# Layer 0's attention: probabilities and values in two f32r parts, products for two query tiles at once, and the queries' fourth partial sum by ScalarE and GpSimd

## The reference

```
w = (qw - 8) * repeat(scales, 128)
q, k, v = x @ w_q, x @ w_k, x @ w_v        # 32 query heads, 8 key/value heads, width 128
q, k = rope(q), rope(k)
scores = q @ k.T / sqrt(128), causal       # per head 1024 x 1024
attn = softmax(scores);  ctx = attn @ v
out = ctx @ w_o                            # summed over the heads
```

## Time and profile before

| | |
|---|---|
| median of 3 runs | 1751.47 us (1750.13 to 1751.73) |
| profiled execution | 1747.66 us |
| its span, first to last instruction | 1745.8 us |
| mean granted TensorE clock | 0.978 |
| busy PE / DVE / ACT / POOL | 95% / 67% / 60% / 43% |
| f32 products of values, L778 | 2304 passes, 299.2 us busy |

### The profile page before, as it was taken

How to read it: one execution, slowest core, us unless ns; L and a number is a source line. 1 busy time by engine, 2 the same in 40 slices (tenths; PEclk the granted TensorE clock), 3 DMA queues, 4 the chain that set the end, 5 groups by cost and what they waited for, 6 DMA issues and landing times. The chain is left out here.

```text
span 1745.8 us, 28527 instructions
## 1 busy us (share of the span) xinstructions
PE 1654.7 (95%) x10107; PEld 1337.1 (77%) x10123; DVE 1170.5 (67%) x2951; ACT 1044.1 (60%) x2261; POOL 747.5 (43%) x705
## 2 busy tenths in 40 slices
PE   4899999999999999999999799999988999999897
PEld 2699989999999989899988488878764555555476
DVE  5767677777777676777666743336777777776285
ACT  3477777877777777777777221114324666666553
POOL 3286585675856757567551300000352334321200
PEclk9999999999999999999999889999979999999998
DMA  6100000101010010000000512200230000000000
GB/s 195 38 14 24 26 25 20 31 13 38 13 31 25 19 37 13 25 19 25 13 19 7 166 46 70 68 1 19 84 83 13 1 1 1 1 1 1 1 19 31
DMA packets 75014, 55.82 MB, mean 32 GB/s; under 512 B 23502, under 2 KB 57998, under 8 KB 74874
## 3 DMA queue, kind: packets, MB, share of 16 engines
q1 hardware_dynamic: 73290, 53.21, 10.5%
q10 hardware_dynamic: 1584, 0.79, 0.2%
HBM read 51.88 MB, written 2.10 MB: 31 GB/s over the span
## 5 line engine op out<-in xcount | busy, mean ns | idle before, releaser
L778 PEld LDWEIGHTS psum<-a_probsT,a_v 128*128 128x128 f32 x2304 | 294.7, 191 | 25.6 <-issue 3.9
L778 PE MATMUL psum<-a_probsT,a_v 128*128 128x128 f32 x2304 | 299.2, 275 | 1.7 <-ACT a_probsT L988 1.6
L877 DVE CUSTOM_DVE_ANT_0 psum<-psum,a_keys_allowed 128x128 f32<-128x128 f32 (+7 forms) x256 | 195.7, 764 | 83.1 <-PE psum L78 74.5
L2109 ACT ACTIVATE a_probsT<-psum 128x512 f32<-128x512 f32 (+1 forms) x304 | 168.4, 588 | 106.1 <-PE psum L1976 67.4
L971 ACT ACTIVATE a_probs<-psum,a_neg_max 128x128 f32<-128x128 f32 (+7 forms) x256 | 190.7, 745 | 66.4 <-DVE a_neg_max L877 58.0
L980 ACT ACTIVATE a_probs<-a_probs,a_row_inv 128x128 f32<-128x128 f32 (+7 forms) x256 | 201.2, 786 | 27.8 <-DVE a_row_inv L884 27.6
L641 POOL TENSOR_TENSOR a_turned_pool<-a_q_sum,a_sine 64x512 f32<-64x512 f32 x62 | 79.3, 1279 | 286.8 <-DVE a_q_sum L863 285.6
L907 DVE TENSOR_TENSOR a_ctxT_lo<-psum,a_ctxT_hi 128x128 fp32r<-128x128 f32 x256 | 73.5, 287 | 172.7 <-ACT a_ctxT_hi L994 172.6
L988 ACT COPY a_probsT<-psum 128x512 f32<-128x512 f32 (+3 forms) x384 | 173.3, 488 | 18.8 <-PE psum L766 16.6
L897 DVE SCALAR_TENSOR_TENSOR a_sumT<-psum,a_scale_o,a_sumT 128x512 f32<-128x512 f32 x248 | 173.5, 741 | 0.9 <-PE psum L792 0.8
L766 PE MATMUL psum<-ident,a_probs 128*128 128x128 f32 x1152 | 168.9, 274 | 0.5 <-ACT a_vT L965 0.3
(11 more groups left out here) (394 smaller groups left out, 3891.3 us busy)
## 6 DMA issues: line engine op xcount, KB each, us to landing
a_raw_o<-in_L_attn_qw_o SPq DMA_DIRECT2D x32, 256.0 KB, 2.8
a_raw_q<-in_L_attn_qw_q SPq DMA_DIRECT2D x31, 256.0 KB, 3.6
mod1b_w<-in_L_wmod SPq DMA_DIRECT2D x4, 1024.0 KB, 6.2
mod0a_w<-in_L_wmod SPq DMA_DIRECT2D x3, 1024.0 KB, 12.8
mod0b_w<-in_L_wmod SPq DMA_DIRECT2D x3, 1024.0 KB, 7.5
f_raw<-in_L_ffn_down_w SPq DMA_DIRECT2D x10, 256.0 KB, 3.1
f_raw<-in_L_ffn_gate_w SPq DMA_DIRECT2D x10, 256.0 KB, 3.3
f_raw<-in_L_ffn_up_w SPq DMA_DIRECT2D x10, 256.0 KB, 3.6
```

The costliest lines, as they stand in the source:

```text
L778: last = nc.tensor.matmul(bank(use)[:, 0:P], v[:, g % 2, j, :], probsT[:, u % 2, j, :], start=(j == 0), stop=(j == i))
L877: nc.vector.tensor_tensor_reduce(out=scores, in0=scores, in1=keys_allowed[:, S - (i + 1) * P:S], scale=-1.0, scalar=-MASKED, op0=ALU.add, ...
L2109: nc.scalar.activation(probsT[:, s % SLOTS, hs[0]:hs[-1] + 1, first:HALF], scores_of(group, n, HALF - first), ACT.Exp).then_inc(exped.sem, 1)
```

## The change

Six things change in this phase:

1. Turned probabilities and v are kept as two f32r parts. ACT copies the high part of the turned probabilities, DVE subtracts it to get the low part (`low_probs`, new). The same is done for v (`high_v` on ACT, `take_v` on DVE).
2. The values of two query tiles are computed together: for pair m, the key tiles 0 to 2m are multiplied as split products 128 x 256 wide; the odd tile's own key tile is done as one f32 product (`own`, a copy of ACT's). The cast and split of values are 256 wide, four a head.
3. The order within a unit: values of a pair (odd units) and the transposes come before the partial products. On DVE the split of values and `low_probs(u-1)` come after `maximum(u+1)` and before the sums, and `invert(u+1)` behind them. On ACT the cast of values and the copy of turned probabilities come right after `exponential(u+1)`. Output products move to even units.
4. A bank of turned probabilities is now taken out when DVE has made the low part (`lowered`).
5. The fourth partial product (k = 3) of the queries from head 2 on is copied with its scale by ACT into `extra` (`take_extra`), and GpSimd adds it to the sum as a first pass of the rope. DVE sums k = 1 and 2 only.
6. To make room, keys and values share one raw buffer, v holds one group, `ctxT` three halves, and some small tiles lie in `sumT`. SP's order of loads follows.

The core of the diff:

```diff
-        return [(h - 1, p - 1), (h - 1, p)] if h > 0 and p % 2 else []
+        return [(h - 1, p), (h - 1, p + 1)] if h > 0 and p % 2 == 0 else []
...
+        if w in (1, 4) and g > 0:
...
+    def pair_due(u):
+        if u % 2 == 0 or u < 3:
+            return []
+        h, i = units[u - 3]
+        return [(h, i // 2)]
...
+        uses += [("pv", *pair) for pair in pair_due(u)]
+        if u > 0:
+            uses += [("t", *piece) for piece in pieces_of(*units[u - 1])]
...
+    by_act_too = lambda key, k: k == KT - 1 and key[0] == "q" and key[1] > 1
+    extras = [key for key, k in partials if by_act_too(key, k)]
...
+            raw = raw_v0 if (name, g) == ("v", 0) else raw_kv
+            if g == 1 and name == "k":
+                sp.wait_ge(*wk_made.of(0))
+            elif g:
+                sp.wait_ge(*(wv_made.of(g - 1) if name == "k" else wk_made.of(g)))
...
+            if key in extras:
+                engine.wait_ge(*extra_out.of(key))
+                compute.tensor_tensor(x, x, extra[:, :], ALU.add).then_inc(counter.sem, 1)
+                engine.wait_ge(*counter.of((key, "extra")))
...
+                if h % REP0 == 0 and g < LAST_GROUP:
+                    load_kv(sp, "v", g + 1)
+                if h % REP0 == 1 and g + 2 <= LAST_GROUP:
                     load_kv(sp, "k", g + 2)
...
                 if kind == "t":
-                    return turned_out.of(name)
+                    return lowered.of(name)
                 key, k = name
+                if key in extras and k == KT - 1:
+                    return extra_out.of(key)
...
+            def values(h, m):
+
+                g, use = h // REP0, ("pv", h, m)
                 wait_bank(use)
-                if h % REP0 == 0 and i % TPH == 0:
-                    pe.wait_ge(*v_taken.of((g, i // TPH)))
-                pe.wait_ge(*turned_out.of(pieces_of(h, i)[-1]))
-                for j in range(i + 1):
-                    last = nc.tensor.matmul(bank(use)[:, 0:P], v[:, g % 2, j, :], probsT[:, u % 2, j, :],
-                                            start=(j == 0), stop=(j == i))
-                last.then_inc(filled.sem, 1)
+                if h % REP0 == 0 and m % 2 == 0:
+                    pe.wait_ge(*v_taken.of((g, m // 2)))
+                pe.wait_ge(*lowered.of(pieces_of(h, 2 * m + 1)[-1]))
+                for j in range(2 * m + 1):
+                    split_products(nc.tensor, bank(use)[:, 0:2 * P], [part[:, j, :] for part in v_parts],
+                                   [part[:, j, :] for part in probsT], j == 0, False)
+                nc.tensor.matmul(bank(use)[:, P:2 * P], v[:, 2 * m + 1, :], own[:, :], start=False, stop=True
+                                 ).then_inc(filled.sem, 1)
...
+                for due in pair_due(u):
+                    values(*due)
+                if u > 0:
+                    turn_probs(u - 1)
                 for due in q_partials(h, p) + kv_partials(h, p):
                     partial(*due)
                 for due in outputs_due(h, p):
                     output(*due)
                 if v_turn(h, p):
                     turn_v(*v_turn(h, p))
-                if u > 1:
-                    values(u - 2)
-                if u > 0:
-                    turn_probs(u - 1)
...
+                tiles_of, turned = slice(b * TPH, (b + 1) * TPH), bank(use).rearrange("p (t d) -> p t d", t=TPH)
+                dve.wait_ge(*v_hi_out.of((g, b)))
+                nc.vector.tensor_copy(v[:, tiles_of, :], turned)
+                nc.vector.tensor_tensor(v_parts[1][:, tiles_of, :], turned, v_parts[0][:, tiles_of, :].bitcast(F32),
+                                        ALU.subtract).then_inc(v_taken.sem, 1)
...
+            def low_probs(u):
+                h, i = units[u]
+                for piece in pieces_of(h, i):
+                    first_key = piece[2] * TPH
+                    keys = slice(first_key, min(first_key + TPH, i + 1 - i % 2))
+                    turned = bank(("t", *piece))[:, 0:(keys.stop - keys.start) * P].rearrange("p (j q) -> p j q", q=P)
+                    dve.wait_ge(*turned_out.of(piece))
+                    nc.vector.tensor_tensor(probsT[1][:, keys, tile(i % 2)], turned, probsT[0][:, keys, tile(i % 2)].bitcast(F32),
+                                            ALU.subtract).then_inc(lowered.sem, 1)
...
+            invert(0)
             for u, (h, i) in enumerate(units):
                 p = u % NT
-                invert(u)
                 if u + 1 < len(units):
                     maximum(u + 1)
                 if u < 2:
                 for use in first_uses(u):
                     if use[0] == "vt":
                         take_v(*use[1:])
+                for due in pair_due(u):
+                    split_values(*due)
+                if u > 0:
+                    low_probs(u - 1)
+                if u + 1 < len(units):
+                    invert(u + 1)
                 for key, k in q_partials(h, p) + kv_partials(h, p):
-                    if k:
+                    if k and not by_act_too(key, k):
                         add_partial(key, k)
                 for due in outputs_due(h, p):
                     add_output(*due)
                 if v_turn(h, p):
                     take_v(*v_turn(h, p))
...
             def take_turned(u):
                 h, i = units[u]
                 for piece in pieces_of(h, i):
-                    c, use = piece[2], ("t", *piece)
-                    keys = min(TPH, i + 1 - c * TPH)
+                    first_key, use = piece[2] * TPH, ("t", *piece)
+                    keys = slice(first_key, min(first_key + TPH, i + 1))
                     act.wait_ge(*filled.of(use))
-                    nc.scalar.copy(probsT[:, u % 2, c * TPH:c * TPH + keys, :].rearrange("p j q -> p (j q)"),
-                                   bank(use)[:, 0:keys * P]).then_inc(turned_out.sem, 1)
-
...
+                    if i % 2 and keys.stop == i + 1:
+                        keys = slice(first_key, i)
+                        nc.scalar.copy(own[:, :], bank(use)[:, tile(i - first_key)])
+                    turned = bank(use)[:, 0:(keys.stop - first_key) * P].rearrange("p (j q) -> p j q", q=P)
+                    nc.scalar.copy(probsT[0][:, keys, tile(i % 2)], turned).then_inc(turned_out.sem, 1)
+
+            def high_values(h, m):
+                use, (n, columns) = ("pv", h, m), part_of_ctx(h, m)
                 act.wait_ge(*filled.of(use))
-                nc.scalar.copy(ctxT[0][:, h % 2, tile(i)], bank(use)[:, 0:P]).then_inc(ctx_hi.sem, 1)
+                nc.scalar.copy(ctxT[0][:, n, columns], bank(use)[:, 0:2 * P]).then_inc(ctx_hi.sem, 1)
...
+            def high_v(g, b):
+                use = ("vt", g, b)
+                act.wait_ge(*filled.of(use))
+                nc.scalar.copy(v_parts[0][:, b * TPH:(b + 1) * TPH, :], bank(use).rearrange("p (t d) -> p t d", t=TPH)
+                               ).then_inc(v_hi_out.sem, 1)
+
+            def take_extra(key):
+                _, n, b = key
+                act.wait_ge(*filled.of(("part", key, KT - 1)))
+                if extras.index(key):
+                    act.wait_ge(*pool_roped.of((extras[extras.index(key) - 1], "extra")))
+                nc.scalar.activation(extra[:, :], bank(("part", key, KT - 1))[:, :], ACT.Copy, scale=scale_of(key, KT - 1)
+                                     ).then_inc(extra_out.sem, 1)
...
                 for use in first_uses(u):
                     if use[0] == "part":
                         take_first(use[1])
+                    elif use[0] == "vt":
+                        high_v(*use[1:])
                     elif use[0] == "so":
...
+                for due in pair_due(u):
+                    high_values(*due)
+                if u > 0:
+                    take_turned(u - 1)
                 for key, k in q_partials(h, p) + kv_partials(h, p):
                     if k == 0:
                         take_first(key)
-                if u > 1:
-                    high_values(*units[u - 2])
-                if u > 0:
-                    take_turned(u - 1)
+                    elif by_act_too(key, k):
+                        take_extra(key)
```

More of the change, by code:

```diff
@@ L458, in layer0_attention_phase @@
     firsts = [use[1] for use in uses if use[0] == "part" and use[2] == 0]
-    added_partials = [partial for partial in partials if partial[1]]
+    by_act_too = lambda key, k: k == KT - 1 and key[0] == "q" and key[1] > 1
+    extras = [key for key, k in partials if by_act_too(key, k)]
+    added_partials = [partial for partial in partials if partial[1] and not by_act_too(*partial)]
     pool_ropes = []
@@ L501, in layer0_attention_phase @@
         summed, ctx_lo, v_taken = count("summed", added_partials), count("ctx_lo", all_values), count("v_taken", v_turns)
+        lowered = count("lowered", pieces)
         ROPE_STEPS = ("sine", "cosine", "sum", "hi", "lo")
```

(11 more changed lines are left out.)

81 lines of the change are left out of this document (33 added, 48 removed).

## The result

| | before | after |
|---|---|---|
| median of the runs | 1751.6 us (1750.13 to 1751.75) | 2065.86 us (2059.26 to 2069.11) |
| ratio | | 1.179, 95% interval [1.176, 1.182] |
| profiled execution: time, span | 1747.66, 1745.8 us | 2069.11, 2067.3 us |
| mean granted clock of the span | 0.978 | 0.933 |

The change costs 314 us. The forecast was 1989 us, with bounds worked out as 1930 and 2045: the direction and the place are right, and the time lies 77 us above the forecast and above the upper bound.

A forecast was written before the change was run, and what follows sets the result against it. TensorE bound the kernel; after, a closed DVE-ACT loop of 34.5 us plus a 1.3 us ring stall makes 35.8 a head. Heads 0 to 28 +217, last heads +19, head 0 +2: +238, so 1989 us, range 1930 to 2045.

The forecast's parts named there:

- TensorE's gain: TensorE's work in a head: split pair products at 0.12 us each, falling by 1.4 us to 26.6 us.
- The loop: DVE and ACT, every unit: maximum, exp, cast, first copy, low_probs, inverse, sums, next maximum; 34.5 us a head.
- The stall of the ring in p=1: Four-bank ring, unit p=1: TensorE's 3.9 us from low_probs against DVE and ACT's 2.6, so 1.3 us a head.
- ACT's cast of a pair: ACT's cast of values in four units a head: about 0.26 us each, 1.0 us a head.
- The term from maximum to exp: From DVE's maximum to the start of ACT's exp: durations of 6.1 plus 0.09 to reach ACT, 6.9 us a head.
- the clock falls: Rival, 10%: TensorE, busy in short pieces, gets a lower clock; +2 to 3 us a head, about 2070 us.
- The last three heads: Heads 28 to 31: 33.2, 31.9 and 30.6 us, together 95.7 where they took 77.1, so +19 us.
- p=7's margin: Unit p=7: TensorE needs about 3.0 us from the end of low_probs, and ACT asks 0.4 us later.
- doubled stalls in p=1 and p=7: At a mean clock of 0.75 the stalls in these two units double: +2 to 3 us a head.
- TensorE as the bound: Rival, 5%: TensorE still sets the time of a head, 45 us less in all, 1707 us.
- Half a loop: Rival, 7%: half of exp and copy on ACT is hidden; 31 us a head, about 1840 us.
- GpSimd's part: The queries' fourth partial sum on ACT (2 x 0.6) and GpSimd (18.2 to 26 us a head, against 35.8): hidden.

The follow-up runs named there:

- experiment 4: Changed kernel with ACT's value casts and turned-probability copies ahead of weighing and exp, and DVE's inverse at the unit's head: 1829.91 us, 1.044.
- experiment 7: Changed kernel plus seventeen needless, overwritten 512-wide products a head on TensorE, ahead of its waits: 2014.06 us, 1.151.
- experiment 7's earlier form: Changed kernel plus fifteen needless products a head, all with the outputs, the last eight behind TensorE's longest wait: 2083.91 us, 1.190.
- experiments 1 and 3: Changed kernel, first with DVE's sums ahead of the low parts: 1958.69 us; third with ACT's copies ahead of exp and DVE's inverse at the unit's head: 1856.13 us.
- experiment 9: Kernel before plus only the fourth partial sum on ACT and GpSimd: 1784.88 us with ACT's copy behind exp, 1753.31 us with it ahead.
- experiment 5: Experiment 4 with exp and weighing first again on ACT in odd units only: 1833.79 us, 1.047.
- earlier low parts (6): Experiment 5 with DVE's low parts ahead of the maximum in even units: 1882.21 us, 1.076.
- an earlier fourth copy (10): Experiment 4 with ACT's copy of the queries' fourth partial sum ahead of exp: 1843.1 us, 1.053.

## Why the prediction was right, and where it was short

**TensorE's gain: its price held.** Products of a pair come 0.12 us apart at full clock (529.74 and 529.86), as worked out. It was worth nothing, since TensorE waits. Nor would it have been worth much: in the best kernel, experiment 4, TensorE is busy for 816.48 of 900 us, 27.8 us of a 30.7 us head, where the kernel before needed 28.04 and the working had 26.6; why the busy time fell by so little, no run told.

**The loop: right, term by term.** Unit by unit from p=0 to p=7, the distances of the maxima. The first column of times is the forecast's terms by unit, with the values' copies as a mean of 0.6 a head left out; the second is experiment 7, at full clock (medians); the third is head 15 of the kernel after, but for p=7, which is the unit just before it (in head 15's own p=7, at full clock, 3.02):

| p | forecast | at full clock | after |
|---|---|---|---|
| 0 | 4.1 | 4.49 | 4.49 |
| 1 | 4.0 | 4.07 | 4.05 |
| 2 | 4.8 | 4.82 | 4.82 |
| 3 | 3.0 | 3.02 | 3.02 |
| 4 | 5.1 | 5.19 | 6.40 |
| 5 | 4.7 | 4.60 | 4.60 |
| 6 | 6.6 | 6.53 | 6.53 |
| 7 | 2.8 | 3.03 | 4.56 |

Low parts of 512 columns took 692 ns; 0.68 to 0.69 had been taken from DVE's other passes. The stall of the ring in p=1, 1.3 us, is in these 4.0; ACT's idle time there was 1.1 us. Two units were clearly short at full clock. One is p=0, by 0.4: DVE waits there for TensorE's output, which the working had as always ready:

```profile
528.82 1.41 DVE L919 SCALAR_TENSOR_TENSOR a_sumT<-psum,a_scale_o,a_sumT 128x512 f32<-128x512 f32 x2 [0.35 <-PE psum L813]
```

The other is p=7, by 0.2. ACT's cast of a pair, 0.26 in the sum, took 0.43 there (523.47 to the copy at 523.90). The term from maximum to exp was added up 0.1 too high: 8 x (0.76 + 0.09) is 6.8.

**The step that failed: the clock.** The forecast's sum held the clock at full, a term of nothing, although the same sum left TensorE idle for 9 us a head. As a rival, "the clock falls" had 10%, at 2 to 3 us a head and about 2070 us. It is what happened: experiment 7 takes it away and a head goes from 38.26 to 36.21 us, 2.05 x 28 = 57 of the 84 us by which the forecast's span was short. The last three heads add 5.5 us (101.9 against 96.4 in experiment 7's earlier form). How it comes about can be read in three views of the kernel after. TensorE at the end of head 12:

```profile
557.91 0.80 PE L812 MATMUL psum<-a_ctxT_lo,a_wo 128*128 128x512 f32 x1 [2.90 <-DVE a_probsT_lo L940]
...
560.64 0.41 PE L77 MATMUL psum<-a_probsT_lo,a_v_hi 128*128 128x256 f32 x1
560.86 0.41 PE L78 MATMUL psum<-a_probsT_hi,a_v_hi 128*128 128x256 f32 x1
```

and the same products 31 us before, in head 12's own p=1:

```profile
529.74 0.28 PE L77 MATMUL psum<-a_probsT_lo,a_v_hi 128*128 128x256 f32 x1
529.86 0.28 PE L78 MATMUL psum<-a_probsT_hi,a_v_hi 128*128 128x256 f32 x1
```

After a wait of 2.90 us for DVE, the products of a pair are 0.22 us apart instead of 0.12: the lower of the two levels, 1.2 instead of 2.4 GHz. The wait alone doesn't settle it: in head 11 TensorE waited 2.79 us in the same place and the clock stayed at 1.00:

```profile
519.89 0.50 PE L812 MATMUL psum<-a_ctxT_lo,a_wo 128*128 128x512 f32 x1 [2.79 <-DVE a_probsT_lo L940]
```

What makes the difference between the two heads, no run told. ACT's value cast in p=7 of heads 11 (full clock) and 12 (low):

```profile
523.47 0.37 ACT L1034 CAST a_ctxT_hi<-psum 128x256 fp32r<-128x256 f32 x1
```

```profile
561.08 0.37 ACT L1008 ACTIVATE a_probs<-psum,a_neg_max 128x128 f32<-128x128 f32 x1 [1.76 <-DVE a_neg_max L899]
...
563.94 0.37 ACT L1034 CAST a_ctxT_hi<-psum 128x256 fp32r<-128x256 f32 x1 [2.41 <-PE psum L800]
```

The first has no idle before it, the second 2.41 us. The prediction had found p=7's margin: "it needs about 3.0 us ... and ACT comes 0.4 later". It took this as slack. At half the clock those 3.0 us outgrow 0.4 of slack, and the unit goes from 3.01 (522.65 to 525.66) to 5.44 us:

```profile
560.70 0.29 DVE L899 CUSTOM_DVE_ANT_0 psum<-psum,a_keys_allowed 128x128 f32<-128x128 f32 x1
...
566.14 0.41 DVE L899 CUSTOM_DVE_ANT_0 psum<-psum,a_keys_allowed 128x256 f32<-128x256 f32 x1
```

The other place is p=4, after a wait of 1.92 us at 585.74: 5.5 us in that head with 5.2 for p=5 behind it (4.6 at full clock), and 6.4 for p=4 in the table's. The forecast looked for doubled stalls in p=1 and p=7; it was p=4 and p=7, while p=1 ran at 1.00. Of the four runs of the kernel after, too, the one with the highest mean clock (0.942) is the shortest (2059.26 us) and the one with the lowest (0.933) the longest (2069.11).

By the Trainium skill's TensorE: Matmul & The Clock Gate, A second HAM failure mode, short idles between groups of matmuls that cycle through banks can make the clock swing. Experiment 7 agrees, at 52 us; the rival deserved more than the 10% given to it.

**The rest of the miss, 26 us.** At full clock a head takes 36.2 instead of 35.8, 11 us in 28 heads, by p=0 and p=7 (v's copies, 2.3 us in one head of four, are 0.57 a head, as counted). The last three heads: 101.9 instead of 95.7, 6 us. That is the clock again: they take 101.9 in experiment 7 too, which left the clock there at 0.93 like after, and 96.4 in its earlier form, at 1.00. The end: 7.0 us, of which 2 lie before the last addition to x (15.6 us after the last maximum, where it was 13.6; 14.1 in that earlier form); the other 5 are in later stages, and no run told them apart. Head 0: 1.5.

**Rivals.** TensorE as the bound is refuted by its idle (80%) and by experiments 1 and 3. Half a loop is refuted by the table by unit. The Trainium skill's rule from Perfetto Trace Analysis, Identifying the Most-Contended Engine, the highest occupancy first, would have made this change 45 us faster; it is 314 slower. (For TensorE that section judges headroom by weight loads and by the rate of arithmetic rather than by the busy time of products; the weight loads were at 746.30 of 825.00 us, 90%, still above ACT's 77%.)

**GpSimd's part: right here, wrong for the kernel before.** "ACT's other work (...) lies in the time in which DVE does low_probs and its sums" is true of the loop. Nothing in the prediction asked who waits for the bank that ACT now empties. In the kernel before, that question is worth 33 us (experiment 9).

**What stays open.** With the loop opened, 78 us over the kernel before are left, 74 of them at 2.6 us a head. TensorE is idle for about as much, 2.8 us a head at full clock (816.48 of 900 us busy). ACT's longest wait isn't their cause (experiment 5), earlier low parts (6) and an earlier fourth copy (10) made it worse. TensorE waits in it for the low parts, its weight loads 72.1 us in all and 1.5 at the longest; which order would free it wasn't found. No version beat the kernel before.

## What to carry to other kernels

Before counting what an edit saves on the fullest engine, write out the order of the two engines that hand work to each other and look for a closed chain through them: here three in-order waits made a loop of 36 us a head out of engines that were at 72 and 77%, and moving ACT's copies ahead of exp, with DVE's inverse, gave back two thirds of the loss. When a loop leaves TensorE idle, price its work once more at half its clock and see which margins are below that; 0.4 us of slack against 3 us of work is none. And where an edit moves the emptying of a shared bank to another engine, ask what stands ahead of it in that engine's queue.

## What the runs showed of the hardware

Seventeen needless products a head made the kernel 52 us faster, by keeping the granted clock at 1.00 where it had been 0.92; they helped ahead of TensorE's waits. Fifteen, with the largest lot behind its longest wait, lost more than they gave in the heads before 28 and gained 5.5 us in the last three. In the kernel after 44 of the 45 low stretches of heads 1 to 31 begin in p=4 or p=6, the units with TensorE's waits of 1.9 and 2.9 us; with the needless products three are left, all from head 28 on. The pattern of low stretches repeats itself with the group of four heads: 38.1, 38.5, 38.0 and 39.0 us (distances of the eight-tile maxima), over and over; with the needless products it is 35.7, 35.7, 38.0 and 35.7. The head of 38.01 to 38.03 is the one with v's copies: it has the most DVE work and still is the shortest, since it runs at 1.00 until its last wait; it is the one that the needless products don't shorten.
